# A third PSUM bank, moved ranks and a moved transpose in the first stage of a vision-tower layer

## What is computed

```python
h = h + mixer(layernorm(h))       # gates = LN(u) @ W_in; scan over time; @ W_out; + x @ W_skip
x = layernorm(h)
logits = x @ gate_w               # 8 experts, the best 2 of each row
shared = silu(x @ sw_gate) * (x @ sw_up) @ sw_down     # hidden width 704
routed = sum over the 2 experts of weight * (silu(x @ w_gate[e]) * (x @ w_up[e])) @ w_down[e]
h = h + routed + shared
```

## Time and profile before

| | |
|---|---|
| median of 3 runs | 1297.93 us (1293.41 to 1303.63) |
| the profiled execution, its time | 1296.02 us |
| its span | 1294.3 us |
| mean granted TensorE clock | 0.946 of full |
| TensorE busy | 1093.9 us, 85% |
| VectorE busy | 860.8 us, 67% |
| ScalarE busy | 354.3 us, 27% |
| GpSimd busy | 387.5 us, 30% |

### The profile page before, as it was taken

One profiled execution on the slowest core, in us unless ns is written; L12 is line 12 of the kernel. 1 busy time (PEld: TensorE's weight loads), 2 busy tenths in 40 slices (PEclk: granted clock), 3 DMA queues, 4 the chain that ended last, 5 costly groups with the idle time before them and its releaser, 6 DMA issues.

```text
span 1294.3 us, 27562 instructions
## 1 busy us (share of the span) xinstructions
PE 1093.9 (85%) x8330; PEld 720.3 (56%) x8331; DVE 860.8 (67%) x2272; ACT 354.3 (27%) x658; POOL 387.5 (30%) x300
## 2 busy tenths in 40 slices
PE   3056899999999999999999996879899999999970
PEld 3045656755775576667666763535555555555530
DVE  7956888888888888898889764524444444444430
ACT  4313324332433243324333432111111111111110
POOL 1000122022212211221122111135455555555650
PEclk8557999999999999999999998989999999999995
DMA  7312133313331333133323349469998877878858
GB/s 242 97 33 67 53 113 138 125 66 117 133 133 66 117 125 137 70 117 116 124 85 125 126 169 407 162 137 189 226 171 134 127 127 132 131 129 132 129 91 268
DMA packets 234736, 174.47 MB, mean 135 GB/s; under 512 B 184434, under 2 KB 203250, under 8 KB 232388
## 3 DMA queue, kind: packets, MB, share of 16 engines
q1 hardware_dynamic: 218148, 128.53, 36.7%
q0 software_dynamic: 15504, 36.46, 14.1%
q10 hardware_dynamic: 1040, 8.91, 1.7%
HBM read 61.59 MB, written 88.12 MB: 116 GB/s over the span
## 4 chain that ended last, share of the span: by engine, by line
PE 51%; DVE 23%; issue 8%; ACT 3%; DMA 3%; SPq 2%; DVEq 1%; POOLq 0%; POOL 0%; ACTq 0%
PE bank L1068 10%; PE bank L1058 9%; PE bank L1059 9%; PE bank L1000 8%; PE bank L919 7%; PE bank L941 5%; DVE wexp L1249 3%; DVE wexp L1270 3%; DVE rows_in L1497 2%; DVE stat L1399 2%; DVE wexp L1229 1%; DVE gf L1277 1%; SPq L754 1%; PE bank L927 1%; DMA x_slots<-x3w,sl 1%
## 5 line engine op out<-in xcount | busy, mean ns | idle before, releaser
L919 PE MATMUL bank<-wexp 128*128 128x256 f16 (+2 forms) x3252 | 416.2, 287 | 30.7 <-DVE gf L1277 15.9
L919 PEld LDWEIGHTS bank<-wexp 128*128 128x128 f16 x3252 | 307.8, 99 | 117.7 <-DVE gf L1277 24.1
L1058 PE MATMUL bank<-wexp,rows_in 128*128 x852 | 256.0, 313 | 10.8 <-issue 4.9
L1059 PE MATMUL bank<-wexp,rows_in 128*128 x852 | 255.4, 313 | 0.0
L897 POOL DMA_INDIRECT sums<-x2w,rows_in x71 | 113.8, 1602 | 124.1 <-DMA sums<-x2w,rows_in 78.9
L1541 DVE SCALAR_TENSOR_TENSOR mixed<-bank,mixed 128x352 f32<-128x352 f32 x71 | 37.2, 525 | 165.3 <-ACT mixed L1206 133.2
L885 POOL TENSOR_TENSOR ex<-base,ld 128x8 f32<-128x8 f32 x71 | 120.5, 1697 | 77.6 <-DVE ld L1520 76.9
L1000 PE MATMUL bank<-wexp 128*128 128x512 f16 x495 | 112.5, 380 | 17.1 <-DVE wexp L1270 15.5
L1058 PEld LDWEIGHTS bank<-wexp,rows_in 128*128 128x128 f16 x852 | 83.2, 98 | 69.5 <-issue 30.3
L864 POOL DMA_INDIRECT x_slots<-x3w,sl x66 | 93.6, 1418 | 88.7 <-DVE sl L1320 44.5
L851 POOL TENSOR_TENSOR inv<-var,power 128x4 f32<-128x4 f32 x17 | 19.1, 1121 | 328.2 <-DVE var L1410 328.2
(11 more groups left out here) (243 smaller groups left out, 1356.8 us busy)
## 6 DMA issues: line engine op xcount, KB each, us to landing
w_halves<-rows_in SPq DMA_DIRECT2D x16, 704.0 KB
wexp<-w_halves ACTq DMA_DIRECT2D x1, 8704.0 KB
wexp<-w_halves SPq DMA_DIRECT2D x8, 1088.0 KB
h_tok<-tokens SPq DMA_DIRECT2D x16, 512.0 KB, 2.6
mixed<-h_tok SPq DMA_DIRECT2D x32, 256.0 KB
sums<-r_o SPq DMA_DIRECT2D x16, 512.0 KB, 2.8
out<-sums SPq DMA_DIRECT2D x16, 512.0 KB, 10.9
x_slots<-zrow SPq DMA_DIRECT2D x8, 792.0 KB, 12.4
```

The costliest lines, as they stand in the source:

```text
L919: last = MM(dst, stat_of(step, a), mov_of(step, b), start=(s_ == 0 and a + b == 0), stop=(s_ == len(steps) - 1 and a == 1))
L1058: MM(GB[:, 0:H], xT[b][:, a, c, :], wexp[:, u, o:o + H], start=s_, stop=e_)
L1059: last = MM(UB[:, 0:H], xT[b][:, a, c, :], wexp[:, u, o + H:o + 2 * H], start=s_, stop=e_)
```

## The change

The groups of gate and up go round three banks (1, 2, 0), so group m waits for the `gprod` of group m - 3. The ranks go to BG in place of BS; their matmuls wait also for `c_th` (the tanh that read BG), `project(0)` no longer waits for `c_sl`, and the transposes of the second tile of x2, which write BG, do. `shared_down(0)` waits for `c_gl` group by group. `rows3(k, 1)` comes behind all three gate projections, and the router waits for each tile's turned rows by itself.

```diff
+        BH = [psum[1], psum[2], psum[0]]
...
-                            at_least(pe, c_gm, n * 6 + m - 1)
-                            bank = BU[m % 2]
+                            at_least(pe, c_gm, n * 6 + m - 2)
+                            bank = BH[m % 3]
...
                                 pe.wait_ge(c_m, n + 1)
-                                MM(BS[:, 256:256 + 2 * E], tri[:], ...
-                                MM(BS[:, 288:288 + 2 * E], ones16[:], ...
+                                if has(k):
+                                    pe.wait_ge(c_th, k + 1)
+                                MM(BG[:, 256:256 + 2 * E], tri[:], ...
+                                MM(BG[:, 288:288 + 2 * E], ones16[:], ...
...
                     def project(i):
                             pe.wait_ge(c_yl, n + 1)
-                            at_least(pe, c_sl, n)
...
                     def shared_down(i):
-                        if i == 0:
-                            pe.wait_ge(c_gl, k * 6)
                         for m in range(SHM):
+                            if i == 0:
+                                pe.wait_ge(c_gl, n * 6 + m + 1)
...
+                        if i == 0:
+                            pe.wait_ge(c_gl, n * 6 + SHM + 1)
                         MM(BD[:], gT[:, SHM, 0, t], wsd[:, SHM, 0, :], start=False, stop=False)
...
                         for q in range(tiles(n)):
+                            if q == 1 and has(k - 1):
+                                pe.wait_ge(c_sl, k)
                             transposes((psum[0], BG)[q], x2r[:, q]).then_inc(c_t2, 2 // tiles(n))
...
-                        if m == 1 and has(k) and tiles(k) == 2:
-                            rows3(k, 1)
+                    if has(k) and tiles(k) == 2:
+                        rows3(k, 1)
                     if has(k):
                         n = k
-                        pe.wait_ge(c_e3, (n + 1) * 2)
                         for i in range(tiles(n)):
+                            pe.wait_ge(c_e3, n * 2 + (i + 1) * 2 // tiles(n))
```

More of the change, by code:

```diff
@@ L974, in body @@
                                 pe.wait_ge(c_m, n + 1)
-                                MM(BS[:, 256:256 + 2 * E], tri[:], m16[:].rearrange("p i e -> p (i e)"), start=True, stop=True)
-                                MM(BS[:, 288:288 + 2 * E], ones16[:], m16[:].rearrange("p i e -> p (i e)"),
+                                if has(k):
+                                    pe.wait_ge(c_th, k + 1)
+                                MM(BG[:, 256:256 + 2 * E], tri[:], m16[:].rearrange("p i e -> p (i e)"), start=True, stop=True)
+                                MM(BG[:, 288:288 + 2 * E], ones16[:], m16[:].rearrange("p i e -> p (i e)"),
                                    start=True, stop=True).then_inc(c_rk, 1)
@@ L1115, in silu @@
                     p1 = P if m < SHM else SHT
-                    A(sgs[P - p1:P, m % 2, 0:w], BU[m % 2][0:p1, 0:w], ACT.Silu, scale=SXW).then_inc(c_sg, 1)
+                    A(sgs[P - p1:P, m % 2, 0:w], BH[m % 3][0:p1, 0:w], ACT.Silu, scale=SXW).then_inc(c_sg, 1)
                 def ghigh(n, m):
@@ L1275, in gprod @@
                     at_least(v, c_gl, n * 6 + m - 1)
-                    u = BU[m % 2][:, TOK:TOK + w] if m < SHM else BU[m % 2][SHT:P, 0:w]
+                    u = BH[m % 3][:, TOK:TOK + w] if m < SHM else BH[m % 3][SHT:P, 0:w]
                     STT(gf[p0:P, m % 2, 0:w], u, SXW, sgs[p0:P, m % 2, 0:w], ALU.mult, ALU.mult).then_inc(c_gm, 1)
@@ L1308, in place @@
                     for i in range(nt):
-                        link(TT(rt[:, 2, i, :], BS[:, 256 + i * E:256 + (i + 1) * E], run[:], ALU.add))
-                        link(TT(run[:], BS[:, 288 + i * E:288 + (i + 1) * E], run[:], ALU.add))
+                        link(TT(rt[:, 2, i, :], BG[:, 256 + i * E:256 + (i + 1) * E], run[:], ALU.add))
+                        link(TT(run[:], BG[:, 288 + i * E:288 + (i + 1) * E], run[:], ALU.add))
                     for c in range(2):
```

## The result

The changed kernel takes 1312.61 us (median of 7 runs, 1306.03 to 1315.46) against 1296.08 us before (7 runs, 1293.41 to 1303.63). The ratio, estimated from all these runs, is 1.0107, with a 95% interval of 1.0081 to 1.0133: about 1% slower (the two medians alone stand 1.0128 apart). Forecast were 1308 us, a chance of 0.63 for a time within 1% of the kernel before, and one of 0.32 for slower by over 1%.

A forecast was written before the change was run, and what follows sets the result against it. The prediction took a loop through VectorE, TensorE and ScalarE to bound the first stage. It summed 1296.0 - 6.2 (waits gone) + 17 (slower clock) = 1306.8, with 1.9 to the median 1308.7, stated as 1308, range 1289 to 1320 us.

The forecast's parts named there:

- What bounds: First-stage body: a loop through VectorE, TensorE and ScalarE sets 43.77 us; TensorE's waits upstream of x2r hold up nothing.
- The pause: Between shared_down(0) and the transposes of x2: TensorE's pauses gather into one of 2.65 us.
- The gain of a held body: First-stage bodies: of 3.1 us gained upstream 0.36 survives, giving bodies of 43.4 us.
- The clock: In the hole before shared_down(1): falls in six bodies in ten, 1.3 us a body, 17 us over 13 bodies.
- The moved rows: Second tile's rows behind the third gate projection: steady bodies stay 0.3 us earlier; the tail loses some 0.2 us each.
- The ends: Body of k = 1 loses a wait of 0.63 us; the last body and tail gain 1.3 us in all.
- Rival 2: Hole before shared_down(1): transposes don't hold the clock, it falls in nearly every body, 2.2 us each, 1320.7 us; chance 0.25.
- Rival 1: First stage: the clock holds despite the pause, 6.2 us less than the median, 1291.7 us; chance 0.25.

The follow-up runs named there:

- e5: Changed kernel with shared_down(1) moved into the pause ahead of the transposes of x2, using the second gate projection's bank; 1289.83 us, ratio 0.9945.
- e6: Changed kernel with the second tile's rows turned behind the second gate projection again, router waits by tile kept; 1316.60 us, ratio 1.0151.
- e2: Changed kernel with 36 more transposes of 128 columns in the pause before the transposes of x2; 1295.17 us, ratio 0.9998.
- e4: Kernel before the change with the third bank alone added; 1296.81 us, ratio 1.0015.

## Why the prediction was right, and where it was off

**The number.** 1312.61 us lies in the range of 1289 to 1320 and 4.6 us above the 1308 forecast, but part of that nearness is luck. The sum was a difference of 10.8 us (1306.8 - 1296.0); measured are 16.5 us between the medians, 13.9 by the ratio and 19.4 between the profiled executions. The median of three runs to which it was tied turned out 1.85 us above that of seven. And of the two outcomes the likelier by the forecast, within 1%, was not the one that the ratio gives, though its interval takes in both.

**What bounds.** Right. The third bank alone gave nothing, and with TensorE's chain shortened the body went to 42.8 us, which had been worked out for e5 from VectorE's waits.

**The pause.** Right to 0.1 us: 2.65 forecast, 2.70 seen; 18.12 us from m = 0 to `shared_down(0)`, as the body of k = 15 showed it.

**The gain of a held body.** 0.36 forecast, 0.2 measured (43.55 against 43.75). The term at fault is the latency from x2r's low half to the transposes, taken as 0.1 us from the row where TensorE waited for `glow`. In the profile after, this half ends at 411.60 and the transposes start at 411.95, 0.35 us. VectorE's row shows that half, with `r_o` right behind it and its wait gone, as forecast:

```profile
410.38 1.22 DVE L1462 SCALAR_TENSOR_TENSOR x2w<-wexp,x2w 128x1024 f16<-128x1024 f32 x1
411.63 0.69 DVE L1468 SCALAR_TENSOR_TENSOR r_o<-bank,h 128x512 f32<-128x512 f32 x1
```

**The clock.** The direction and the price of a fall were right: 45.33 - 43.55 = 1.78 us against 1.7 plus a rare longer one. What was mis-sized is the share: 6 in 10 assumed, 10 in 12 found (and in the bodies of k = 1 and 14 too). It had been taken from four stretches of the trace before, three of which fell, and set lower than those; four were too few. The two errors, 0.83 x 1.78 = 1.48 us against 1.3 and 0.2 against 0.36, make 1.3 us a body where 0.94 was forecast. (The forecast's own 0.6 x 1.7 + 0.1 x 3.4 is 1.36, rounded down there to 1.3.)

**The moved rows.** The path was as forecast (a router's pause of 0.83 us between the tiles, 0.45 us of its work done ahead), and they cost nothing (e6).

**The ends.** The tail gained 1.5 us, near the 1.3 forecast. The 0.63 us of k = 1 did not come. Its second projection waits 0.70 us less for h, but its twelve matmuls take 4.74 us against 2.76, since the clock fell there too; the body is 1.6 us longer:

```profile
144.10 4.74 PE L920 MATMUL bank<-wexp 128*128 128x512 f16 x12 [1.68 <-DVE h L1480]
```

**Rival 2** had the right place and nearly the right share, at too high a price (2.2 us a body against 1.48) and for a reason that e2 speaks against: 36 transposes do hold the clock. The stretch of 98.8 to 102.2 could not decide that, since the two others that were as empty (1.02 us busy of 3.40) were followed by a fall too. Rival 1, the clock that holds, is what the fillings made of the kernel; it too comes out less fast than forecast, by 0.16 us a body (0.2 gained, not 0.36) and by what the fillings cost in the body of k = 14.

## What to carry to other kernels

When TensorE's waits lie upstream of something that another engine brings later, taking them away gains nothing and gathers them into one pause: work out how long the new pause is and look in the trace what the granted clock did around pauses of that length. Scattered waits of up to 1.1 us kept the clock at 1.00 here, and so did one of 1.9 us between matmuls (e4); the same 2.7 us in one piece cost 1.7 us or more in ten bodies of twelve. The remedy is useful work in the pause, `shared_down(1)` in this case, which also shortens the chain; but look at the next longest pause then, since in e5 the clock fell there. Matmuls whose result nobody reads give back only the clock.

## What was not expected of the hardware

Transposes alone (36 of 128 columns) kept the granted clock at 1.00 as ten matmuls of 512 columns did. And equal pauses don't have equal ends: ahead of the transposes of x2, the clock fell at 1.9 us in exactly each second body, at 2.7 us in ten of twelve, at 2.9 us in all.
